# Four transformer-like graph layers on one core: the 32-wide layer's projections in three products, rearranged engine sequences and a regrouped set-up

## What is computed

```
x = layernorm(x + L0(x, adj))   # masked attention, 4 heads of 64
x = layernorm(x + L1(x, adj))   # 4 heads: tanh(adj * (Wh attn Wh^T)) Wh, relu, A_w, gated with fc
x = layernorm(x + L2(x, adj))   # 8 heads of 32: masked softmax * (cosine > 0.1), graph convolution
x = layernorm(x + L3(x, adj))   # masked attention as layer 0, other weights
```

## Time and profile before

| | |
|---|---|
| median of the runs | 2848.74 us |
| profiled execution, its own time | 2851.96 us |
| its span (first to last instruction) | 2850.2 us |
| mean granted TensorE clock | 0.983 |
| instructions | 61579 |
| weights, inputs and outputs moved | 29.76 MB |

### The profile page before, as it was taken

One profiled execution on the slowest core, in us unless ns is written; L12 is line 12 of the kernel. 1 busy time (PEld: TensorE's weight loads), 2 busy tenths in 40 slices (PEclk: granted clock), 3 DMA queues, 4 the chain that ended last, 5 costly groups with the idle time before them and its releaser, 6 DMA issues. The chain is left out here.

```text
span 2850.2 us, 61579 instructions
## 1 busy us (share of the span) xinstructions
PE 2669.7 (94%) x21265; PEld 2335.4 (82%) x21265; DVE 1991.9 (70%) x6621; ACT 1381.5 (48%) x3841; POOL 939.0 (33%) x971
## 2 busy tenths in 40 slices
PE   4789999999999999999999999999999999999985
PEld 3778888888888888888888888888888888888873
DVE  3347767777776777777677777767777776777764
ACT  0234545545454554555455445545544554554442
POOL 0033333323333333334333333433333343333321
PEclk9799999999999999999999999999999999999997
DMA  3000000000000000000000000000000000000000
GB/s 120 5 6 2 11 11 10 9 8 2 9 9 9 9 9 4 6 9 9 9 9 9 0 9 9 9 9 9 9 0 9 9 9 9 9 9 0 9 5 8
DMA packets 44480, 29.76 MB, mean 10 GB/s; under 512 B 21264, under 2 KB 44048, under 8 KB 44432
## 3 DMA queue, kind: packets, MB, share of 16 engines
q1 hardware_dynamic: 44432, 29.13, 3.5%
HBM read 20.73 MB, written 8.39 MB: 10 GB/s over the span
## 5 line engine op out<-in xcount | busy, mean ns | idle before, releaser
L176 POOL TENSOR_SCALAR l_ve<-l_mv 128x2 f32<-128x2 f32 x128 | 42.6, 333 | 1048.7 <-DVE l_mv L161 1048.6
L1229 ACT ACTIVATE b<-b,s_sh 128x256 f32<-128x256 f32 x512 | 255.6, 505 | 109.7 <-DVE s_sh L418 109.7
L245 PE MATMUL bank<-a32r 128*128 128x256 f32 x1024 | 304.4, 297 | 3.6 <-issue 2.2
L1480 POOL TENSOR_TENSOR a32r<-a,a32r 128x512 fp32r<-128x512 f32 x128 | 180.9, 1413 | 339.8 <-ACT a32r L1179 337.4
L247 PE MATMUL bank<-a32r 128*128 128x256 f32 x1024 | 289.6, 283 | 0.0
L246 PE MATMUL bank<-a32r 128*128 128x256 f32 x1024 | 289.2, 282 | 0.0
L1485 POOL TENSOR_TENSOR a32r<-a,a32r 128x512 fp32r<-128x512 f32 x128 | 166.4, 1300 | 301.7 <-ACT a32r L1175 301.7
L418 DVE CUSTOM_DVE_ANT_0 b<-bank,s_add 128x256 f32<-128x256 f32 x512 | 185.9, 420 | 84.5 <-issue 59.2
L413 DVE TENSOR_TENSOR a32r<-bank,a32r 128x512 fp32r<-128x512 f32 x128 | 85.6, 689 | 208.2 <-ACT a32r L1216 114.9
L245 PEld LDWEIGHTS bank<-a32r 128*128 128x128 f32 x1024 | 195.2, 191 | 37.3 <-issue 22.9
L1388 DVE SCALAR_TENSOR_TENSOR b<-bank,b 128x256 f32<-128x256 f32 x512 | 188.2, 420 | 33.5 <-PE bank L1083 31.3
(11 more groups left out here) (248 smaller groups left out, 8777.2 us busy)
## 6 DMA issues: line engine op xcount, KB each, us to landing
x_in<-in_x SPq DMA_DIRECT2D x32, 256.0 KB, 2.8
out<-x SPq DMA_DIRECT2D x32, 256.0 KB, 2.1
adj_a<-in_adj SPq DMA_DIRECT2D x32, 64.0 KB, 2.5
adj_b<-in_adj SPq DMA_DIRECT2D x32, 64.0 KB, 2.5
b<-in_L_gnn_A_w SPq DMA_DIRECT2D x1, 1024.0 KB, 7.3
a<-in_L_gnn_W SPq DMA_DIRECT2D x4, 256.0 KB, 5.3
a<-in_L_gnn_attn SPq DMA_DIRECT2D x4, 256.0 KB, 5.1
g_b_wh<-in_L_gnn_bW SPq DMA_DIRECT2D x1, 512.0 KB, 8.3
```

Of the source, the lines that this page charges most:

```text
L176: pool.tensor_scalar(N.ve[:, :], N.mv[:, :, 1], LN_EPS, None, ALU.add).then_inc(N.eps.sem, 1)
L245: pe.matmul(out, w[0], x[0], start=first, stop=False)
L1229: last = act.activation(S.e[:, n, it, :], S.e[:, n, it, :], ACT.Exp, bias=S.sh[:, it, h:h + 1], scale=-1.0, accum_out=S.sums[:, it, h:h + 1])
L1480: pool.tensor_tensor(G.wh[h % 2][1], G.whf[:, h % 2, :, :], G.wh[h % 2][0].bitcast(F32), ALU.subtract).then_inc(G.wh_sb.sem, 1)
```

## The change

It does the following.

- The four projections of layer 2 take their weights as pairs (`split_sb`) and their input as a pair `S.xt` in a new buffer `b32r`. ScalarE's b_x_t copy writes the high half, a new stage b_x_t on VectorE (83 stages now) the low half; the projection stages now run through the three-product branch.
- `ORDER` is new for all engines. The sets of stages are otherwise the same. g_ha_3_1 and g_ha_3_0 move from the end of a turn to the beginning of the next, d_q as well.
- The buffers of layer 0 (`A.e`, `A.pt`, `A.qt`, `A.kt`, `A.v`) are placed over those of layer 1, through a float32 and a float32r name for the same bytes (`arena`, `arena_r`).
- ScalarE's g_wh of heads 2 and 3 has a further wait, for the product g_p of two heads before.
- In the set-up the loads stand in groups with semaphores of their own: g (W, A_w), a (attn, fc, g1, g2), s (the layer-2 weights, gcn_W and the small columns), r (layer 0's and 3's weights and the spread biases), the last behind x and the masks of graph 0. TensorE waits for each group where it first needs it. ScalarE makes the high halves, VectorE the low halves and the plain copies; GpSimd halves the four layer-0 weights. The order of TensorE's steps is changed: fc's product no longer waits for the transposes of map, q and k, and the column products stand earlier.

The diff, cut:

```diff
     "PE": [
-        ("g_gate_x", 1), ("a_x_t", 0), ("g_ha_t", 1), ("d_k", 2), ("g_gate", 1), ("d_scores_0", 2), ("d_v", 2),
-        ("a_q", 0), ("a_k", 0), ("d_scores_1", 2), ("a_scores_0", 0), ("a_v", 0), ("d_probs_0", 2), ("d_probs_1", 2),
-        ("a_scores_1", 0), ("d_probs_2", 2), ("d_probs_3", 2), ("b_x_t", 1), ("d_values_0", 2), ("d_values_1", 2),
-        ("a_probs_0", 0), ("a_probs_1", 0), ("a_probs_2", 0), ("a_probs_3", 0), ("a_values_0", 0), ("a_values_1", 0),
-        ("d_out", 2), ("a_out", 0), ("b_m", 1), ("g_adj_t", 0), ("b_k", 1), ("b_sem", 1), ("g_x_t", 0), ("b_q", 1),
-        ("g_z_0", 0), ("b_unit_t", 1), ("g_c", 0), ("b_scores_0", 1), ("g_z_1", 0), ("g_wh_0", 0), ("g_s_0", 0),
...
-        ("g_p_2", 0), ("b_values_1", 1), ("g_ha_1_1", 0), ("g_ha_2_1", 0), ("b_out", 1), ("g_p_3", 0),
-        ("g_ha_1_0", 0), ("g_ha_2_0", 0), ("g_hf", 0), ("g_ha_3_1", 0), ("d_x_t", 1), ("g_ha_3_0", 0), ("d_q", 1),
+        ("g_ha_3_1", 1), ("g_ha_3_0", 1), ("d_k", 2), ("g_ha_t", 1), ("a_x_t", 0), ("g_gate_x", 1), ("d_q", 2),
+        ("g_gate", 1), ("d_scores_0", 2), ("d_v", 2), ("a_k", 0), ("d_scores_1", 2), ("a_q", 0), ("a_v", 0),
+        ("a_scores_0", 0), ("d_probs_0", 2), ("d_probs_1", 2), ("d_probs_2", 2), ("d_probs_3", 2), ("a_scores_1", 0),
+        ("d_values_0", 2), ("b_x_t", 1), ("a_probs_0", 0), ("a_probs_1", 0), ("d_values_1", 2), ("a_probs_2", 0),
+        ("a_probs_3", 0), ("a_values_0", 0), ("a_values_1", 0), ("d_out", 2), ("a_out", 0), ("b_m", 1), ("b_sem", 1),
+        ("g_adj_t", 0), ("b_q", 1), ("g_x_t", 0), ("b_k", 1), ("g_z_0", 0), ("b_unit_t", 1), ("g_c", 0),
+        ("b_scores_0", 1), ("g_wh_0", 0), ("g_z_1", 0), ("g_s_0", 0), ("b_cos_0", 1), ("g_wh_1", 0), ("g_s_1", 0),
+        ("b_transpose_0", 1), ("b_transpose_1", 1), ("b_transpose_2", 1), ("b_transpose_3", 1), ("g_wh_2", 0),
+        ("b_values_0", 1), ("g_z_2", 0), ("b_scores_1", 1), ("g_p_0", 0), ("g_s_2", 0), ("g_z_3", 0), ("b_cos_1", 1),
+        ("g_p_1", 0), ("b_transpose_4", 1), ("g_wh_3", 0), ("b_transpose_5", 1), ("b_transpose_6", 1), ("g_s_3", 0),
+        ("b_transpose_7", 1), ("g_p_2", 0), ("b_values_1", 1), ("g_hf", 0), ("b_out", 1), ("g_ha_0_1", 0),
+        ("g_ha_0_0", 0), ("g_ha_1_1", 0), ("g_ha_1_0", 0), ("g_p_3", 0), ("g_ha_2_0", 0), ("g_ha_2_1", 0),
+        ("d_x_t", 1),
     ],
     "ACT": [
+        ("b_copy_6", 2), ("g_wh_3", 1), ("g_p_2", 1), ("g_s_3", 1), ("b_relu_1", 2), ("g_a_3", 1), ("g_p_3", 1),
...
+        ("d_probs_2", 2), ("a_exps_0", 0), ("a_exps_1", 0), ("a_exps_2", 0), ("a_exps_3", 0), ("a_probs_0", 0),
+        ("b_x_t", 1), ("a_probs_2", 0), ("a_o_copy", 0), ("g_x_t", 0), ("b_k", 1), ("b_q", 1), ("g_z_0", 0),
...
+        ("b_relu_0", 1), ("g_z_2", 0), ("g_a_1", 0), ("b_exps_4", 1), ("g_wh_2", 0), ("g_p_0", 0), ("g_s_2", 0),
...
     ],
     "DVE": [
+        ("b_factors", 2), ("b_copy_5", 2), ("b_copy_7", 2), ("g_p_2", 1), ("g_a_3", 1), ("b_scale", 2), ("b_sum", 2),
+        ("b_stats", 2), ("b_norm_out", 2), ("g_p_3", 1), ("g_diff", 1), ("a_x_t", 0), ("g_ha_t", 1), ("g_gate", 1),
+        ("d_mask_0", 2), ("g_mix", 1), ("d_v", 2), ("g_sum", 1), ("d_mask_1", 2), ("g_stats", 1), ("d_mask_2", 2),
+        ("d_norm_p_0", 2), ("d_mask_3", 2), ("a_v", 0), ("g_norm_out", 1), ("d_norm_p_1", 2), ("a_mask_0", 0),
+        ("a_mask_1", 0), ("d_probs_1", 2), ("a_mask_2", 0), ("a_mask_3", 0), ("a_norm_p_0", 0), ("d_probs_3", 2),
+        ("a_norm_p_1", 0), ("a_probs_1", 0), ("a_probs_3", 0), ("d_o_copy", 2), ("b_x_t", 1), ("a_o_copy", 0),
+        ("d_sum", 2), ("a_sum", 0), ("a_stats", 0), ("b_m", 1), ("b_square", 1), ("a_norm_out", 0), ("d_stats", 2),
+        ("g_x_t", 0), ("b_sem", 1), ("b_unit", 1), ("g_z_0", 0), ("g_c", 0), ("b_mask_0", 1), ("b_mask_1", 1),
+        ("b_mask_2", 1), ("g_wh_0", 0), ("b_mask_3", 1), ("g_z_1", 0), ("g_adj_t", 0), ("b_cut_0", 1), ("b_cut_1", 1),
+        ("b_cut_2", 1), ("b_cut_3", 1), ("g_wh_1", 0), ("g_a_0", 0), ("b_copy_1", 1), ("b_copy_3", 1), ("g_a_1", 0),
+        ("g_wh_2", 0), ("g_z_2", 0), ("b_mask_4", 1), ("b_mask_5", 1), ("b_mask_6", 1), ("b_mask_7", 1), ("g_p_0", 0),
+        ("d_norm_out", 2), ("g_a_2", 0), ("b_cut_4", 1), ("b_cut_5", 1), ("g_z_3", 0), ("b_cut_6", 1), ("g_p_1", 0),
+        ("b_cut_7", 1), ("g_wh_3", 0),
     ],
     "POOL": [
+        ("g_wh_2", 2), ("g_a_2", 2), ("b_sums", 3), ("g_wh_3", 2), ("g_a_3", 2), ("b_mask", 2), ("b_rstd", 3),
...
     ],
...
+        arena = sb("arena", [P, ARENA * T * NODES])
+        arena_r = nc.alloc_sbuf_tensor_at("arena_r", [P, ARENA * T * NODES], F32R, offset=ARENA_AT)
...
-        a32, a32r = places("a32", 10, F32), places("a32r", 22, F32R)
-        b32 = places("b32", 13, F32)
-
-        x1 = a32(9)
+        a32, a32r, plain = places("a32", 5, F32), places_of(arena_r), places_of(arena)
+        b32, b32r = places("b32", 13, F32), places("b32r", 2, F32R)
+
+        x1 = a32(4)
         A = attention_layer(ctx, nc, "l0", BA, x1, split=True)
         D = attention_layer(ctx, nc, "l3", BB, x3, split=False)
-        A.e, A.pt, A.qt, A.kt, A.v, A.xb = a32(0, 4), a32(4, 4), a32(4), a32(5), a32(8), x1
+        A.e, A.pt, A.qt, A.kt, A.v, A.xb = plain(10, 4), plain(16, 4), plain(14), plain(15), plain(8), x1
         A.xt, A.ot = split(a32r, 2), split(a32r, 4)
...
-        S.m, S.sq, S.u, S.xt, S.sem = (b32(n) for n in (4, 5, 6, 7, 0))
+        S.m, S.sq, S.u, S.sem = (b32(n) for n in (4, 5, 6, 0))
+        S.xt = split(b32r, 0)
...
-        S.w_m, S.w_q, S.w_k, S.w_s = (sb(f"s_w_{n}", [P, T, DIM])[:, :, :] for n in "mqks")
+        S.w_m, S.w_q, S.w_k, S.w_s = (split_sb(f"s_w_{n}", [P, T, DIM]) for n in "mqks")
...
+        loads_g = [(W.w[:, h, :, :], rows(d["L1_gnn_W"][h])) for h in range(HG)] + whole((W.a_w, "L1_gnn_A_w"))
+        loads_a = [(W.attn[:, h, :, :], rows(d["L1_gnn_attn"][h])) for h in range(HG)]
+        loads_a += whole((W.fc, "L1_gnn_fc_w"), (W.g1, "L1_gnn_g1_w"), (W.g2, "L1_gnn_g2_w"))
+        loads_s = whole((W.map, "L2_gnn_map_w"), (W.q, "L2_gnn_q_w"), (W.k, "L2_gnn_k_w"), (W.gm, "L2_gnn_gcn_map_w"))
+        loads_r = whole((W.wq, "L0_gnn_Wq"), (W.wk, "L0_gnn_Wk"), (W.wv, "L0_gnn_Wv"), (W.wo, "L0_gnn_Wo"))
+        columns_s = [(W.bw[:, :, h], column(d["L1_gnn_bW"][h])) for h in range(HG)]
+        columns_s += [(t[:, :], column(d[n])) for t, n in (
             (W.mb, "L2_gnn_map_b"), (W.qb, "L2_gnn_q_b"), (W.kb, "L2_gnn_k_b"), (W.gb, "L2_gnn_gcn_map_b"))]
-        loads += [(t[:, :], spread(ap)) for t, ap in (
+        loads_r += whole((D.wq, "L3_gnn_Wq"), (D.wk, "L3_gnn_Wk"), (D.wv, "L3_gnn_Wv"), (D.wo, "L3_gnn_Wo"))
+        loads_r += [(t[:, :], spread(ap)) for t, ap in (
             (A.bo, d["L0_gnn_bo"]), (D.bo, d["L3_gnn_bo"]), (S.b_m, d["L2_gnn_map_b"]), (G.b_gate, d["L1_gnn_gbias"]),
             (G.b_wh, d["L1_gnn_bW"].rearrange("h o -> (h o)")))]
-        n_loads = len(loads) + P // DHS
...
+            pe.wait_ge(const_ready, 5)
+            pe.wait_ge(wg_loaded, 16 * len(loads_g))
+            for h in range(HG):
+                step(lambda b: pe_transpose_rows(pe, b, W.w[:, h, :, :], C.ident))
+            for cc in range(HG):
+                step(lambda b: pe_transpose_rows(pe, b, W.a_w[:, :, cc * DIM:(cc + 1) * DIM], C.ident))
+            pe.wait_ge(wa_loaded, 16 * len(loads_a))
+            for h in range(HG):
+                r_done = step(lambda b: mm_pairs(b, W.attn[:, h, :, :], lambda kc: W.w[:, h, kc, :]))
+            for h in range(HG):
+                step(lambda b: mm_pairs(b, W.w[:, h, :, :], lambda kc: W.r[:, h, kc, :]), needs=r_done)
+            for src in (W.fc, W.g2, W.g1):
+                g1_done = step(lambda b: pe_transpose_rows(pe, b, src, C.ident))
+            pe.wait_ge(ws_loaded, 16 * n_s)
+            for src in (W.map, W.q, W.k):
+                t_done = step(lambda b: pe_transpose_rows(pe, b, src, C.ident))
+            gcn_done = step(lambda b: pe.transpose(b[:, 0:P], W.gcn, C.ident[:, :]))
+            step(lambda b: mm_pairs(b, W.fc, lambda kc: W.g1_t[:, kc, :]), needs=g1_done)
             a_done = step(lambda b: columns(b, lambda h, kc, t: W.attn[:, h, kc, t * P:(t + 1) * P],
                                             lambda h, kc: W.bw[:, kc, h:h + 1], HG))
+            step(lambda b: columns(b, lambda h, kc, t: W.r[:, h, kc, t * P:(t + 1) * P], lambda h, kc: W.bw[:, kc, h:h + 1], HG))
+            step(lambda b: mm_pairs(b, W.map, lambda kc: W.q_t[:, kc, :]), needs=t_done)
+            step(lambda b: mm_pairs(b, W.map, lambda kc: W.k_t[:, kc, :]))
+            b_q_done = step(lambda b: columns(b, lambda h, kc, t: W.q_t[:, kc, t * P:(t + 1) * P], lambda h, kc: W.mb[:, kc:kc + 1], 1))
+            step(lambda b: columns(b, lambda h, kc, t: W.k_t[:, kc, t * P:(t + 1) * P], lambda h, kc: W.mb[:, kc:kc + 1], 1))
+            step(sem_weight, needs=gcn_done)
+            step(sem_bias, needs=b_q_done)
             step(lambda b: columns(b, lambda h, kc, t: W.w[:, h, kc, t * P:(t + 1) * P],
```

(46 more changed lines are left out.)

177 lines of the change are left out of this document (77 added, 100 removed), and 19 rows, old and new, of the table ORDER.

## The result

The changed kernel takes 2782.7 us (median of 4 runs, 2778.7 to 2785.2) against 2848.9 us for the kernel before (4 runs): a ratio of 0.977, 95% interval 0.975 to 0.978, some 66 us faster. The prediction was 2769.0 us with a range of 2742 to 2808. The profiled execution took 2784.76 us, span 2782.9 us; against the 2851.96 us of the execution that the sum was made against it is 67.2 us less, where the sum said 80.

A forecast was written before the change was run, and what follows sets the result against it. TensorE's instruction order was taken to set the loop's clock, other engines mattering only where it waits. Gains of 39 + 12 + 27 + 2 = 80 us off 2851.96, less 3.2, gave 2769 us, range 2742 to 2808.

The forecast's parts named there:

- the forecast's own case: Whole kernel: the main forecast of 2769 us, with a turn of 81.2 to 82.3 us; chance 0.60.
- Part 1: Layer 2's four projections in the loop: 12 float32r matmuls each instead of 8 records, 1.27 us a turn, 39 us.
- Rival A: Loop: waits take back the products, turn stays at 83.35 us, only set-up and drain gain, 2820 us; chance 0.12.
- Part 2: VectorE in the loop: one more 0.69 us subtraction a turn fits into idle time and costs nothing.
- Part 3: Rearranged sequences in the loop: TensorE's waits fall from 2.4 to about 2.0 us a turn, 12 us in all.
- Part 4: Set-up: earlier TensorE start 23 us, shorter wait for VectorE 2.5, ScalarE's table load 1.3; sum 27 us (16 to 32).
- Part 5: Prologue and drain: the last graph's projections get shorter, VectorE's 0.69 us goes on top; 2 us gained (0 to 5).
- B: Loop: the new order sheds nearly all TensorE waits, turn 79.85 us, 2712 us, or 2740 half of the way; chance 0.13.
- C: Loop: the new VectorE subtraction delays a_o_copy and a_out, making the kernel slower, 2868 us at 3.2 us a turn; chance 0.03.
- D: Set-up: does not shorten as planned, 10 us gained instead of 27, 2786 us; chance 0.07.
- E: Projections in the loop: weight loads bind, half of the products' gain is lost, 20 us, 2789 us; chance 0.05.

The follow-up runs named there:

- the early b_m: Changed kernel with projection b_m moved ahead of a_out, d_out behind it, and VectorE doing b_m and the squares ahead of a_sum: 2769.2 us.
- the one-wait kernel: Changed kernel, but TensorE waits for all four groups of loads before its first set-up step: 2808.5 us.
- the last kernel: On top of the early b_m: d_norm_out behind g_a_1, d_rstd behind b_inorm, and hidden-bias columns moved behind the 32-wide layer's fourth weight in the set-up: 2751.6 us.

## Why the prediction was right, and where its steps failed

The total came out 14 us above the forecast. Two errors in the loop cancelled by less than half: 39 us for the products and 12 for the order were forecast, 10 and 25 came, and the set-up gave 4 more than forecast. The range reached 39 us up, so it would have held the error of the products alone. That the total lay inside it says little for the mechanism. The turn of 82.39 us lies just outside the 81.2 to 82.3 of the forecast's own case.

**Part 1, the products: forecast 39 us (34 to 46), measured 10.3 and 10.5.** The bare work was close. With the waits taken out, the plain four take 6.88 us a turn (1.73 + 1.73 + 1.78 + 1.64) and the new four about 5.86 (1.41 + 1.41 + 1.52 + 1.52): 1.0 us, 31 us in all, instead of 1.27. The prediction read the 12 matmuls from chains at 0.113 and 0.118 us; they run at 0.117 to 0.118 us in all four. And b_sem's 1.89 us held 0.16 us of lateness hidden by the modelled ends. What failed is the step from work to time: I priced the saving as if TensorE alone set the length of that stretch, though the same text knew of g_x_t's wait for layer 0 and called it gone. In the changed kernel it is 0.35 us late, and g_z_0 0.20. Rival A (waits take back the products), at 0.12, names what happened to most of this term: 29 of the 39 us did not come, 8 of them because the work saved was smaller, the rest as waits. Its turn of 83.35 us did not come, and the waits stood at layer 0's normalisation and not where it put them. With the wait ahead of g_x_t removed the products brought 23 to 25 us (the two kernels with a_norm_out between the halves of b_square), and the early b_m gave the changed kernel 10 us of what the wait had taken.

**Part 2, VectorE's subtraction at nothing: right** (a second one: 2781.0 against 2782.7 us).

**Part 3, the order: forecast 12 us, measured 24.6 and 24.9.** The wait at d_x_t went as said, the one at d_probs_2 went further than the 0.4 to 0.7 us that I had left of it, the one at a_scores_1 went as said. Waits came as said, but 0.2 us shorter each, at d_values_0 (0.3) and a_probs_0 (0.5), by the record. The one at g_x_t, called gone, stayed, and new ones that I had not looked for stand at b_transpose_4 and, with 0.2, at a_scores_0. In sum the recorded waits went from 2.4 to 1.6 us. Counted by lateness, as above for g_x_t, they are by my estimate about 3.3 us a turn before and 2.7 after: the recorded ones were too small a base. With plain products the order gained 0.60 us a turn, 18.6 us, and another 6 us in the first two turns, which the prediction had not priced: 74.0 and 78.9 us in the old order, 68.6 and 77.2 in the new one, probably since g_ha_3 and d_q now belong to the next turn; no run tests that.

**Part 4, the set-up: forecast 27 us (16 to 32), measured 31.2.** The start at 10.03 us against 10.5; 23.8 us by the one-wait kernel against 23. TensorE's wait for VectorE ahead of fc's product, 3.92 us, is 0.48 us, and all its waits inside the set-up fell by 4.7 us, where 2.5 (0 to 4) was forecast. ScalarE's share of that is 3.0 us, by the kernel in which VectorE casts. The table load's 1.3 us were put into the wrong sum: it stood behind the first x_in transpose (94.01 us), so its gain lies in the first turn, outside the 31.2. The 3.0 us that are left are of the size of one row of columns: n_ac with w took 6.99 us at half clock before and takes 4.00 now. That is the clock, which was forecast at 0 with 3 us both ways.

**Part 5, the drain: forecast 2 us, measured nothing.** 183.2 and 183.4 us at granted clocks of 0.87 and 0.86. Why its shorter projections do not show was not tried. The changed kernel and the two with its loop and another set-up have drains of 182.7 to 184.8 us, so a gain of 2 us could hardly be seen.

**Rivals.** B's full shedding of waits did not come. C is refuted by the doubled subtraction, D by 31.2 us. E, weight loads: their busy time in a turn is 70.75 us against 70.87, the b_m and b_sem chains run at 0.118 us a matmul, and the products gain 23 us once the wait is out: not a bound here. The turn of 82.39 us was inside the limits (80.8 to 82.8) outside which I would have called the prediction wrong, and so would have hidden the two errors; only the parts undone one at a time showed them.

## What to carry to other kernels

A saving on the bound engine counts only as far as no chain through other engines spans the stretch it is in: before pricing it, measure the chain (here 7.0 us from a_out's end to g_z_0) against the engine's own work in between, and fill the chain with work that was cheap to move. Count lateness as start minus the start that the spacing allows, not as recorded idling. Where moving one instruction only moves the wait, look at the whole queue of the engine waited for, and in it for the instruction whose time is not its own. Moving such an instruction helps only as far as the one that takes its place can bear the same delay.

## What the runs showed of the hardware that was not expected

**TensorE's half clock in the set-up lasts differently long in executions of the same instructions.** The same stretch of the set-up in the changed kernel, then in the kernel with the early b_m, whose set-up is the same, then in the kernel in which VectorE makes the casts (columns as in the earlier trace rows, the granted clock is third from the end):

```profile
40.00:53.00 13.00, 13.00 (x49) 11.81 (x49) 1.02 (x3) 0.60 (x1) 6.50 (x7) 0.51 0.00 1
```

```profile
40.00:53.00 13.00, 13.00 (x74) 12.18 (x73) 2.15 (x8) 1.75 (x3) 6.45 (x7) 0.74 0.01 1
```

```profile
40.00:53.00 13.00, 13.00 (x64) 13.00 (x62) 1.55 (x3) 0.00 (x0) 7.49 (x8) 0.50 0.00 0
```

The first two fall to 0.5, that is 1.2 instead of 2.4 GHz, during the 64 one-column products that begin at about 36 us, at about 39 and 41 us. In the first the half clock lasts until about 53 us, in the second until about 48, and x_in's first transpose comes at 57.0 instead of 61.6 us. These 4.6 us are part of the 15.5 us between the two profiled executions and not the edit's. The prediction had this at 0 with 3 us both ways. In the last kernel the 32 n_bw,b columns stand elsewhere, and the fall comes at about 47 us, again among columns:

```profile
44.70 4.42 PE L740 MATMUL bank<-n_bw,b 128*128 128x1 f32 x32
48.98 1.20 PE L733 MATMUL bank<-b 128*128 128x128 f32 x4
49.98 6.83 PE L740 MATMUL bank<-n_ac,a 128*128 128x1 f32 x32
```

The clock is 0.84 over 46 to 48 us and 0.50 from 48 to 56 us there; at full clock 32 columns took 3.63 us, the last 32 here 6.83. TensorE is busy throughout, so in these kernels the fall does not come at an idle moment. That the columns bring it is not shown, and one kernel speaks against it. Where VectorE casts, the clock is at half from about 38 us, ahead of the first column and 1 us behind a wait of 2.02 us:

```profile
36.94 3.12 PE L720 MATMUL bank<-arena 128*128 128x256 f32 x8 [2.02 <-DVE arena L798]
39.85 6.83 PE L740 MATMUL bank<-n_bw,arena 128*128 128x1 f32 x32
```

A set-up without such columns was not tried, so the cause stays open.

**A VectorE instruction from SBUF to SBUF can take nearly three times its time beside GpSimd**: 2.05 us for 0.73, in every turn in the middle of the run. The kernel before had it too, unseen in the prediction: in the turn of the earlier trace rows the normalisations of layers 1 to 3 take 1.13, 1.48 and 1.13 us. Which of the two engines loses depended, in the two kernels read above, on who came first.
